# A selective-scan layer on one core: the input term u made by TensorE for all states, and y summed untransposed

## The reference, cut to what matters

```python
x     = silu(conv(resid_norm @ W_in) + conv_b)             # E = 1024 channels
delta = softplus(x @ W_delta_1 @ W_delta_2 + b_delta_2)
Bm, Cm = x @ W_B, x @ W_C                                   # N = 16 states
A = -exp(A_log)
def step(h, inp):                                           # over the 2048 rows
    A_bar = exp(d_l[:, :, None] * A)
    h = h * A_bar + (d_l * x_l)[:, :, None] * B_l[:, None, :]
    y_l = einsum('ben,bn->be', h, C_l)
ys, then (y + x * W_D) * silu(resid_norm @ W_skip), then resid + that @ W_out
```

## Time and profile before

| what | value |
|---|---|
| device time, median of 3 runs | 2380.34 us (2379.85 to 2382.69) |
| device time of the profiled execution | 2379.91 us |
| its span | 2378.0 us |
| busy: PE, DVE, ACT, POOL | 82%, 75%, 70%, 80% of the span |
| granted TensorE clock, mean | 0.939 of full speed |
| HBM traffic | 182 GB/s over the span |

### The profile page before, as it was taken

One profiled execution on the slowest core, in us unless ns is written; L12 is line 12 of the kernel. 1 busy time (PEld: TensorE's weight loads), 2 busy tenths in 40 slices (PEclk: granted clock), 3 DMA queues, 4 the chain that ended last, 5 costly groups with the idle time before them and its releaser, 6 DMA issues. The chain is left out here.

```text
span 2378.0 us, 35550 instructions
## 1 busy us (share of the span) xinstructions
PE 1958.7 (82%) x11717; PEld 1584.2 (67%) x11717; DVE 1795.4 (75%) x3105; ACT 1669.1 (70%) x3276; POOL 1913.5 (80%) x1192
## 2 busy tenths in 40 slices
PE   5577777898889898898889898898889988797883
PEld 3456666777667676777667686776667776666551
DVE  3377877798697977888697977889697887887522
ACT  2368686877769685787779686786868687787421
POOL 1279898898789797989879897998879898999512
PEclk9988988999999999999999999999999999999996
DMA  4555556665747565674657556574757646555320
GB/s 159 169 178 182 189 177 215 201 216 157 225 151 239 180 215 183 203 229 150 210 175 235 196 186 215 185 228 148 232 169 222 194 154 207 181 183 160 120 71 18
DMA packets 239281, 434.31 MB, mean 183 GB/s; under 512 B 19134, under 2 KB 135418, under 8 KB 239098
## 3 DMA queue, kind: packets, MB, share of 16 engines
q1 hardware_dynamic: 239098, 432.04, 56.9%
HBM read 347.57 MB, written 84.41 MB: 182 GB/s over the span
## 5 line engine op out<-in xcount | busy, mean ns | idle before, releaser
L608 POOL TENSOR_TENSOR hc<-h,c_all 128x1024 f32<-128x1024 f32 x512 | 1205.0, 2365 | 219.5 <-DVE h L953 160.0
L953 DVE TENSOR_TENSOR_SCAN h<-operand,carry,bank 128x512 f32<-128x512 f32 x480 | 597.1, 1271 | 174.1 <-PE bank L1129 142.7
L1134 PE MATMUL y_sum<-ident,hc 128*128 128x128 f32 x4096 | 624.7, 281 | 13.0 <-POOL hc L608 12.7
L1129 PE MATMUL bank<-ident,u_t 128*128 128x128 f32 x2560 | 417.3, 288 | 243.2 <-DVE h L953 219.7
L722 ACT ACTIVATE u_t<-dx_t,b_t 128x256 f32<-128x256 f32 x1280 | 575.0, 499 | 0.5 <-PE bank L1129 0.5
L1129 PEld LDWEIGHTS bank<-ident,u_t 128*128 128x128 f32 x2560 | 312.4, 148 | 375.1 <-issue 240.2
L1134 PEld LDWEIGHTS y_sum<-ident,hc 128*128 128x128 f32 x4096 | 506.1, 146 | 79.8 <-issue 50.2
L592 POOL TENSOR_TENSOR operand<-dx_q,b_all 128x1024 f32<-128x1024 f32 x192 | 454.5, 2367 | 11.0 <-DMA b_all<-bc_dram 11.0
L703 ACT ACTIVATE bank<-delta_q,neg_a 128x512 f32<-128x512 f32 x384 | 262.5, 684 | 263.1 <-DVE h L953 262.7
L703 ACT ACTIVATE operand<-delta_q,neg_a 128x512 f32<-128x512 f32 x640 | 432.9, 714 | 0.0
L953 DVE TENSOR_TENSOR_SCAN h<-bank,carry,operand 128x512 f32<-128x512 f32 x288 | 354.9, 1270 | 33.1 <-POOL operand L592 16.4
(11 more groups left out here) (124 smaller groups left out, 2009.3 us busy)
## 6 DMA issues: line engine op xcount, KB each, us to landing
c_all<-bc_dram SPq DMA_DIRECT2D x256, 512.0 KB, 4.3
b_all<-bc_dram SPq DMA_DIRECT2D x192, 256.0 KB, 5.2
win<-in_L_attn_W_in SPq DMA_DIRECT2D x64, 512.0 KB, 5.7
wskip<-in_L_attn_W_skip SPq DMA_DIRECT2D x64, 512.0 KB, 6.2
x_dram<-x SPq DMA_DIRECT2D x64, 256.0 KB, 4.5
delta_dram<-delta SPq DMA_DIRECT2D x32, 512.0 KB, 7.3
dx_dram<-dx SPq DMA_DIRECT2D x32, 512.0 KB, 7.3
delta_q<-delta_dram SPq DMA_DIRECT2D x32, 512.0 KB, 5.8
```

The costliest lines, as they stand in the source:

```text
L608: nc.gpsimd.tensor_tensor(hc[:, number % 3], h[:, number % 3], c_all[:, j % 2, s % 2:s % 2 + 1].to_broadcast([P, 2, SPAN]), ALU.mult).then ...
L953: nc.vector.tensor_tensor_scan(h[:, number % 3, q], first, second, start, ALU.mult, ALU.add).then_inc(scan_done.sem, 1)
L1129: last = transpose(bank[:, q, b * P:(b + 1) * P], u_t[:, j % 2, b, q * P:(q + 1) * P], ident[:])
L1134: return matmul(to, lhsT=of, rhs=ident[:], is_transpose=True, start=start, stop=stop, skip_group_check=True)
```

## The change

u of all sixteen states is now made in one way. ACT scales the identity by a column of B, four 128x128 diagonals for each slot, in a ring of four (`diag_b`). PE multiplies the turned dx with these diagonals into `bank`, four real 128x128 products for each q. POOL's `make_u`, the rows of B and their loads, and ACT's `u_t` are gone. The decays always go to an SBUF ring of four, `decays`, and `bank` is written by PE alone. ACT makes diagonals three slots ahead (two before) and decays two slots ahead (one before). `y_sum` now has channels on the partitions: each slot adds hc with one real 128x512 product against the identity for each q. y is stored and loaded in that form, so the transposes of `acc` into `mixed` are gone; the gate is computed in place in `routed`, and ys is their product with `acc`. PE's first W_in product of a step and the turning of dx move one or two slots earlier, the second half of W_out one slot later.

```diff
@@ SP
-                        load_b(step, slot + 4)
-                    sp.dma_start(b_all[:, j % 2], bc_dram[stage % 2, n:n + 1].to_broadcast([P, SPAN])).then_inc(
-                        b_loaded[j % 2].sem, 16)
@@ POOL
-                    nc.gpsimd.tensor_tensor(operand[:, number % 3], dx_q[:, k],
-                                            b_all[:, j % 2:j % 2 + 1].to_broadcast([P, 2, SPAN]),
-                                            ALU.mult).then_inc(u_ready.sem, 1)
-                        make_u(step, slot + 2)
@@ ACT, decay
-                    if turned_u(n):
-                        if v := due(act, scan_done, t, 2 * (s - 2)):
-                            act.wait_ge(scan_done.sem, v)
-                        to = operand[:, number % 3, q]
-                    else:
-                        if v := due(act, scan_done, t, 2 * (s - 1) + q + 1):
-                            act.wait_ge(scan_done.sem, v)
-                        to = bank[:, q]
+                    if v := due(act, scan_done, t, 2 * (s - 3)):
+                        act.wait_ge(scan_done.sem, v)
-                    nc.scalar.activation(to, delta_q[:, k, q], ACT.Exp,
+                    nc.scalar.activation(decays[:, number % 4, q], delta_q[:, k, q], ACT.Exp,
@@ ACT, make_ut / make_diag
-                    if v := due(act, ut_turned, t, 2 * j - 2):
-                        act.wait_ge(ut_turned.sem, v)
+                    if v := due(act, u_turned, t, 2 * (s - RING + 1)):
+                        act.wait_ge(u_turned.sem, v)
                     for b in (2 * pair, 2 * pair + 1):
-                        last = nc.scalar.activation(u_t[:, j % 2, b], dx_t[:, k, b], ACT.Copy,
+                        last = nc.scalar.activation(diag_b[:, number % RING, b], ident[:], ACT.Copy,
                                                     scale=b_t[:, stage % 2, b, n:n + 1])
@@ ACT, order in a slot
-                        make_ut(step, slot + 2, 0)
-                        decay(step, slot + 1, 0)
-                        make_ut(step, slot + 2, 1)
-                        decay(step, slot + 1, 1)
+                        make_diag(step, slot + 3, 0)
+                        decay(step, slot + 2, 0)
+                        make_diag(step, slot + 3, 1)
+                        decay(step, slot + 2, 1)
@@ DVE
-                        nc.vector.tensor_tensor_scan(h[:, number % 3, q], first, second, start, ALU.mult,
+                        nc.vector.tensor_tensor_scan(h[:, number % 3, q], decays[:, number % 4, q], bank[:, q], start, ALU.mult,
                                                      ALU.add).then_inc(scan_done.sem, 1)
@@ PE, turn_u
                     for b in range(SB):
-                        last = transpose(bank[:, q, b * P:(b + 1) * P], u_t[:, j % 2, b, q * P:(q + 1) * P],
-                                         ident[:])
-                    last.then_inc(ut_turned.sem, 1)
+                        last = matmul(bank[:, q, b * P:(b + 1) * P], dx_t[:, k, b, q * P:(q + 1) * P],
+                                      diag_b[:, number % RING, b], start=True, stop=True)
+                    last.then_inc(u_turned.sem, 1)
@@ PE, add_y
-                    for b in (2 * pair, 2 * pair + 1):
-                        for q in range(2):
-                            last = add_turned(y_sum[:, b, q * P:(q + 1) * P], hc[:, number % 3, q, b * P:(b + 1) * P],
-                                              False, n == N - 1)
-                    if pair:
+                    last = matmul(y_sum[:, q], lhsT=ident[:], rhs=hc[:, number % 3, q], start=False, stop=n == N - 1)
+                    if q:
                         last.then_inc(hc_read.sem, 1)
@@ PE, side work
-                    if late and slot in (27, 29):
-                        turn_dx(step + 1, 0, slot // 29)
+                    if (slot, late) in ((27, 0), (28, 1)):
+                        turn_dx(step + 1, 0, late)
-                                            last = transpose(mixed[:, (2 * e + b) * P:(2 * e + b + 1) * P],
-                                                             acc[:, p % 2, b, e * P:(e + 1) * P], ident[:])
```

More of the change, by code:

```diff
@@ L46 @@
 NORMED = 8
+RING = 4
 class Signal:
@@ L97, in jobs_of @@
     return tuple(job for job, chunk in ahead.items() if 0 <= chunk < CHUNKS)
[L100 to L111, removed]
 def build(nc, resid, norm_w, w_skip, w_in, conv_w, conv_b, w_delta_1, w_delta_2, b_delta_2, w_b, w_c, a_log,
@@ L164, in build @@
         dx_t = sb("dx_t", P, 2, SB, QE)
-        b_all, c_all = sb("b_all", P, 2, SPAN), sb("c_all", P, 2, 2, SPAN)
-        operand = sb("operand", P, 3, 2, SPAN)
-        u_t = sb("u_t", P, 2, SB, QE)
+        c_all = sb("c_all", P, 2, 2, SPAN)
+        decays = sb("decays", P, 4, 2, SPAN)
+        diag_b = sb("diag_b", P, RING, SB, P)
         h, hc = sb("h", P, 3, 2, SPAN), sb("hc", P, 3, 2, SPAN)
         carry = sb("carry", P, N, ET)
-        y_out = sb("y_out", P, SB, QE)
-        acc = sb("acc", P, 2, TB, QE)
-        thg, gate = sb("thg", P, 2, 2, T), sb("gate", P, 2, 2, T)
+        y_out = sb("y_out", P, 2, SPAN)
+        acc = sb("acc", P, 2, 2, T)
+        thg = sb("thg", P, 2, 2, T)
         ys = sb("ys", P, ET, T)
@@ L741, in take_y @@
                         act.wait_ge(y_stored.sem, v)
-                    for pair in range(2):
-                        part = slice(2 * pair, 2 * pair + 2)
-                        nc.scalar.activation(y_out[:, part], y_sum[:, part], ACT.Copy,
-                                             scale=0.5).then_inc(y_read.sem, 1)
+                    for q in range(2):
+                        nc.scalar.activation(y_out[:, q], y_sum[:, q], ACT.Copy, scale=0.5).then_inc(y_read.sem, 1)
                 for et in range(ET):
@@ L751, in _ @@
                     for slot in range(SLOTS):
-                        if slot == 31:
-                            take_dxt(step + 1, 0, 1)
                         if slot == 2:
@@ L757, in _ @@
                             take_y(step, 0)
-                        if slot == 29:
-                            take_dxt(step + 1, 0, 0)
+                        if slot in (29, 30):
+                            take_dxt(step + 1, 0, slot // 30)
                         if slot in (11, 13):
@@ L939, in scan @@
                         dve.wait_ge(carry_saved.sem, v)
-                    if not turned_u(n):
-                        if v := due(dve, u_ready, t, before(PLAIN_STATES, s) + 1):
-                            dve.wait_ge(u_ready.sem, v)
                     for q in range(2):
@@ L946, in scan @@
                             dve.wait_ge(exp_ready.sem, v)
-                        first, second = bank[:, q], operand[:, number % 3, q]
-                        if turned_u(n):
-                            if v := due(dve, ut_turned, t, 2 * before(TURNED_STATES, s) + q + 1):
-                                dve.wait_ge(ut_turned.sem, v)
-                            first, second = second, first
+                        if v := due(dve, u_turned, t, 2 * s + q + 1):
+                            dve.wait_ge(u_turned.sem, v)
                         start = 0.0 if stage % STAGES_PER_BATCH == 0 else carry[:, n, et:et + 1]
-                        nc.vector.tensor_tensor_scan(h[:, number % 3, q], first, second, start, ALU.mult,
+                        nc.vector.tensor_tensor_scan(h[:, number % 3, q], decays[:, number % 4, q], bank[:, q], start, ALU.mult,
                                                      ALU.add).then_inc(scan_done.sem, 1)
@@ L1120, in turn_u @@
                     t, s = now
-                    if not turned_u(place(t, s)[2]):
-                        return
-                    j = before(TURNED_STATES, s)
-                    if v := due(pe, ut_ready, t, j + 1):
-                        pe.wait_ge(ut_ready.sem, v)
+                    k, number = place(t, s)[3:]
+                    if v := due(pe, diag_ready, t, s + 1):
+                        pe.wait_ge(diag_ready.sem, v)
+                    if v := due(pe, dxt_ready, t, 2 * k + 2):
+                        pe.wait_ge(dxt_ready.sem, v)
                     if v := due(pe, scan_done, t, 2 * (s - 1) + q + 1):
@@ L1174, in turn_dx @@
                     if k:
-                        for read, step in ((gate_ready, t - 1), (o_ready, t - 1)):
+                        for read, step in ((ys_ready, t - 1), (o_ready, t - 1)):
                             if v := due(pe, read, step, read.per):
@@ L1247, in side_work @@
                             for p in range(PAIRS):
-                                if (s, late) in ((3 * p - 2, 1), (3 * p - 1, 0)):
-                                    e = s - 3 * p + 2
+                                first = 3 * p - 2 if p else -3
+                                if (s, late) in ((first, 1), (first + 1, 0)):
+                                    e = s - first
                                     if v := due(pe, rnt_ready, t - 1, 2):
```

127 lines of the change are left out of this document (36 added, 91 removed).

## The result

The changed kernel takes 3015.03 us (median of 4 runs, 3013.58 to 3016.68), the one before 2380.1 us (4 runs, 2378.74 to 2382.69). The ratio is 1.2666, with a 95% interval of 1.2644 to 1.2688: 26.7% slower. The forecast was 3011 us.

What follows compares the result with a forecast made beforehand. PE's full queue was taken to bound the changed kernel: 127 us start, 2673 us PE work, 60 us stalls and 149 us tail, plus 1.9 us outside the span, gave 3011 us. The range was 2945 to 3105 us.

Steps and rivals of the forecast that it cites:

- The bound: Middle stretch: PE work grows from 1642 to 2673 us, over the present 2102 us, so PE becomes the bound.
- rival that the hand-overs keep their price: Middle stretch: PE doesn't fill, hand-overs cost what they do, 1031 us come on top: 3411 us; chance 0.09.
- The cost of an instruction: On PE: a real float32 product is two records, a transpose one; 0.111 us per 128x128 record, 0.43 per 128x512.
- rival with one record for each product: Not slower: u and y products on PE pass as one record each, about 2310 us; chance 0.02.
- The stalls: Middle stretch: waits for scans, the wait for `dx_q` and one per cent for hand-overs, together about 60 us.
- the wait for `dx_q`: In PE's queue in every second step: 3 us each, 24 us, between 0 and 78.
- PE's waits for scans: Long slots of the middle stretch: the one with 0.44 us of side work stalls some 0.5 us, 14 times.
- my 27: Middle stretch: one more per cent for hand-overs, an estimate of 27 us.
- The range: Whole time, 2945 to 3105 us: lower end without stalls, upper with clock at 0.95 and `dx_q` wait at its bound.
- The clock at 0.95: Middle stretch: mean clock stays 0.95, 2673 becomes 2814, time 3092 us without other stalls; no chance of its own given.
- The tail: The part after the middle stretch, without scans: 149 us, left as it is.
- Start, ACT, POOL, DVE: Start 127 us unchanged; POOL near 1460, ACT near 1800 us; ACT's wait for bank, DVE's for POOL's u go, hidden.

Runs made afterwards that it cites:

- four plain states: Kernel before with POOL making u of four states (0, 5, 8, 13) in place of six: 2366.15 us, ratio 0.9934.
- four, one of them moved: Kernel before with POOL making u of four states, 6 in place of 5 (0, 6, 8, 13): 2370.11 us, ratio 0.9957.
- two plain states: Kernel before with POOL making u of two states (0, 8) in place of six: 2434.96 us, ratio 1.0235.
- all turned: Changed kernel with u of all states by ACT scaling and PE transposes, y by transposes, no real product in either: 2511.98 us, ratio 1.055.
- the same, half of ACT's scaling: The all turned kernel with half of ACT's scalings of dx left out, PE's work the same: 2444.6 us, ratio 1.0275.
- y alone: Kernel before with y summed by real 128x512 products and acc not turned, u made as before: 2540.57 us.
- transposes for u, product for y: Changed kernel with u of all states scaled by ACT and turned by PE transposes, y still by real products: 2676.55 us.
- u alone: Changed kernel with y summed by transposes as before and acc turned again, u by real products: 2713.34 us.
- decays in SBUF alone: Kernel before with all decays in an SBUF ring of three and POOL's u in its own buffer: 2690.7 us; with PE's earlier turn in bank: 2647.03 us.
- the last two runs: Changed kernel with POOL's 192 products put back as useless work, 3016.13 us; and with diagonals two and decays one slot ahead, 3014.73 us.

## Why the prediction was right, point by point

**The bound.** That PE's queue fills and then sets the time held. The kernels by PE work, middle stretch, the rest that isn't PE work, and PE's idle time by the busy time of the stretch (us):

| kernel | PE work | middle | rest | PE idle |
|---|---|---|---|---|
| before | 1642 | 2102 | 460 | 312 |
| four plain states | 1698 | 2087 | 389 | 263 |
| four, one of them moved | 1698 | 2091 | 393 | 254 |
| two plain states | 1755 | 2164 | 409 | 259 |
| all turned | 1811 | 2231 | 420 | 264 |
| the same, half of ACT's scaling | 1811 | 2161 | 350 | 215 |
| y alone | 2046 | 2259 | 213 | 127 |
| transposes for u, product for y | 2215 | 2389 | 174 | 114 |
| u alone | 2269 | 2434 | 165 | 102 |
| after | 2673 | 2726 | 53 | 17 |

The two kernels with decays in SBUF alone aren't in it: their scans are longer, and with 1642 us of PE work their middle stretches take 2414 and 2371 us. The rest isn't all waiting: the part of it in which PE is busy is 148 us before, at a granted clock of 0.95, and 36 us after, at 1.00.

Up to 1811 us of work the time isn't read from PE's work alone: 1698 is faster than 1642, and two kernels with 1811 are 70 us apart. Above 2000 it is PE's work and a rest that shrinks as the queue fills. The step from the last but one row to the last adds 404 us of work and 292 us of time. The rival that the hand-overs keep their price (3411) is gone with it.

**The cost of an instruction.** Records and distances were as read: 8192 at 0.111 and 2048 at 0.43. This was the step on which all hung, and it decides between 2310 and 3011. The rival with one record for each product has no support.

**The stalls.** Predicted 60 us in the middle, measured 53 (2726 - 2673). The parts were less well placed: the wait for `dx_q` 2.0 us where I took 24, PE's waits for scans 14.5 us where I took 7. The remaining 36 us, against my 27, is time in which PE is busy beyond records times distance, not a stall, and no run took it apart. The sum came out by luck more than by its terms. In the kernels with u alone and with transposes for u, 60 us as in the prediction was short by 105 and 114 us: the stalls grow as the queue gets less full, and the prediction had no term for that.

**The range.** Its upper end doesn't follow from its reasons. The clock at 0.95 alone gives 3092, and with the `dx_q` wait at its bound of 78 us it would be 3170, not 3105. Neither came: the clock was 1.00, the wait 2.0 us.

**The tail** was taken as unchanged, and it is 13 us longer. The chain near the end, in the changed kernel:

```profile
2871.26 6.53 PE routed L1227 x16
2880.07 5.39 PE routed L1227 x16
2887.75 3.71 PE routed L1227 x16
```

Sixteen records of W_skip take 3.71 us at the full clock. Here two of three such groups take 5.39 and 6.53, at a granted clock of 0.68 and 0.56 while they run, and 0.86 over that part of the tail (0.95 before). Two parts of the change meet here. The transposes of `acc`, which stood between these groups, are gone. And since the gate is computed in place in `routed`, the next W_skip group waits for ys and not for the gate: PE waits 17.1 us for it in the tail, where it waited 8.7. The kernels with one part each tell them apart. With the `acc` transposes gone and the gate in its own tile (y alone) the tail is 152 us; with the wait for ys and `acc` turned (u alone, all turned) 150.5 and 152; with both (transposes for u, after) 159 and 162. So neither part costs more than about 3 us by itself, and both together cost 10 to 13: longer idle times with less work between them, and groups at a lower clock behind them.

**Start, ACT, POOL, DVE.** ACT came to 1766.7 us (about 1800 said), POOL to 1479.5 (near 1460), both hidden, as the last two runs show for POOL's work and ACT's lead. That ACT's wait for `bank` and DVE's wait for POOL went wasn't tried by itself in the changed kernel; with PE idle for 17 us of the middle stretch, there is hardly more than that to gain.

What stays open: of the 132 us by which all states turned is slower than before, about half goes with half of ACT's scaling. For the other half, DVE now depends on PE in every slot (it waits 440.9 us for `bank`, 191.1 before), but no run took this apart.

## What to carry to other kernels

Count PE work in records and their distance, not in instructions: here a float32 product of 128x128 takes two records of 0.111 us and a float32 transpose one, and one 128x512 product (0.86 us) is hardly cheaper than four of 128x128 (0.89). Work moved to the busiest engine first fills its slack and costs less than its length (160 us for 404 in y alone); once that engine is full, its work is the time, and what is freed elsewhere is worth nothing. Add the candidate's work to the busy time of its stretch before writing it. Where DVE and POOL run side by side, an operand that stands in PSUM may be what keeps them apart: look at the longest duration of an instruction, not only at its mean.

## What the runs showed of the hardware that I had not expected

- A `tensor_tensor_scan` of 128x512 with both operands in SBUF takes 1.19 to 3.38 us beside POOL's two-input products, and ends 1.08 to 1.12 us after the product that ran when it began; with one in PSUM it takes 1.19 to 1.29. The kernel with 384 such scans is 13% slower.
- The granted clock of the middle stretch was 1.00 in the changed kernel, where PE is idle for 17 us of it, and 0.95 before, where it is idle for 312. In the kernel with all states turned, an idle time of 4.96 us on PE was followed by four transposes in 1.08 us at a clock of 0.50, where they take 0.60 at 1.00.
- With all waits met, groups of different form follow one another on PE without a gap: 1.75 us for u and y of one q, in the changed kernel, is 8 x 0.111 + 2 x 0.43.
